# Row maxima in row tiles of the array, all row sums by additions, and a shared ring of banks

## The reference

```python
xn = _layernorm(x)                                   # x: (8, 1024, 512) float32
q, k, v = proj(Wq, bq), proj(Wk, bk), proj(Wv, bv)   # 16 heads of 32
scores = jnp.einsum('bhid,bhjd->bhij', q, k) / jnp.sqrt(32)
im = jnp.arange(L) % 256
scores = jnp.where(im[:, None] >= im[None, :], scores, -1e30)
attn = jnp.einsum('bhij,bhjd->bhid', jax.nn.softmax(scores, axis=-1), v)
s = attn.transpose(0, 2, 1, 3).reshape(B, L, D) @ Wo.T + bo
w = (weights >= 0.0) * 2.0 - 1.0
g = _silu(jnp.clip((xn @ w.T) * scale + bias, -100, 100))
out = x + s * g
```

## Time and profile before

| | |
|---|---|
| median of three runs | 1720.07 us (1716.95 to 1721.70) |
| span of the profiled execution | 1718.3 us (the profile has no time outside it) |
| PE busy | 1670.7 us, 97% |
| DVE, POOL, ACT busy | 1344.2, 1188.0, 1158.4 us |
| POOL additions L1205 | 763.9 us in 628 |
| DVE maxima L1008 | 780.6 us in 1216 |
| ACT exponentials L796 of transposed scores | 621.6 us in 1088 |

### The profile page before, as it was taken

The page is one execution under the profiler, slowest core; times in us unless marked ns, Lnnn a source line. Parts: engine busy times, 40 slices in busy tenths (PEclk is TensorE's granted clock), DMA queues, the critical chain, the costliest instruction groups (busy, mean ns, idle before and its releaser), DMA issues.

```text
span 1718.3 us, 34103 instructions
## 1 busy us (share of the span) xinstructions
PE 1670.7 (97%) x11660; PEld 781.8 (45%) x11660; DVE 1344.2 (78%) x2641; ACT 1158.4 (67%) x2734; POOL 1188.0 (69%) x1186
## 2 busy tenths in 40 slices
PE   8999999999999999999999999999999999999988
PEld 4444444444444444444444444444444444444433
DVE  6889677787778877888777877778777787777874
ACT  4577676677677765677756777666776677666763
POOL 0167667786867768777588775787757786667775
PEclk9999999999999999999999999999999999999989
DMA  7314212333123421234122331224312332122111
GB/s 212 110 39 88 69 45 63 87 89 85 34 71 92 100 57 46 68 99 100 38 63 69 104 85 37 75 63 111 76 38 64 81 99 54 42 63 75 44 51 50
DMA packets 185038, 126.09 MB, mean 73 GB/s; under 512 B 106912, under 2 KB 159264, under 8 KB 184416
## 3 DMA queue, kind: packets, MB, share of 16 engines
q1 hardware_dynamic: 183904, 123.13, 28.2%
q10 hardware_dynamic: 960, 0.79, 0.2%
HBM read 41.50 MB, written 17.05 MB: 34 GB/s over the span
## 4 chain that ended last, share of the span: by engine, by line
PE 83%; ACT 7%; DVE 5%; issue 2%; POOL 1%; DMA 1%; ACTq 0%; SPq 0%; POOLq 0%; DVEq 0%
PE pJ L496 29%; PE pO L698 15%; PE pS L655 11%; PE pT L679 10%; PE pT L675 3%; PE pJ L588 3%; PE pJ L592 3%; PE pJ L589 3%; ACT pS L808 3%; PE pS L658 3%; DVE mx L1008 2%; ACT PT L796 2%; PE pT L639 2%; PE pJ L583 1%; ACT acc L796 1%
## 5 line engine op out<-in xcount | busy, mean ns | idle before, releaser
L1008 DVE TENSOR_REDUCE mx<-pS 128x1 f32<-128x512 f32 (+3 forms) x1216 | 780.6, 656 | 258.0 <-PE pS L655 176.0
L796 ACT ACTIVATE PT<-pT 128x512 f32<-128x512 f32 (+1 forms) x1088 | 621.6, 583 | 431.1 <-PE pT L679 381.6
L1205 POOL TENSOR_TENSOR acc<-acc,PT 128x512 f32<-128x512 f32 x628 | 763.9, 1250 | 30.3 <-PE pO L698 30.3
L655 PE MATMUL pS<-QK 96*128 96x512 f16 (+3 forms) x1280 | 389.7, 318 | 20.1 <-ACT pS L808 14.5
L679 PE MATMUL pT<-QK 97*128 97x512 f16 (+3 forms) x1280 | 393.4, 318 | 4.2 <-ACT PT L796 1.6
L808 ACT ACTIVATE pS<-pS,a 128x384 f32<-128x384 f32 (+3 forms) x512 | 266.1, 524 | 13.8 <-DVE a L1023 13.4
L698 PE MATMUL pO<-PT,V 128*32 128x512 f32 (+3 forms) x2816 | 262.4, 486 | 0.2 <-ACT PT L796 0.2
L655 PEld LDWEIGHTS pS<-QK 96*128 96x128 f16 x1280 | 124.4, 98 | 166.0 <-issue 44.4
L496 PE MATMUL pJ<-xT,wh_q 128*128 128x512 f16 x512 | 191.7, 379 | 2.2 <-ACT xT L737 1.7
L496 PE MATMUL pJ<-wh_v,xT 128*128 128x512 f16 x512 | 192.5, 379 | 0.8 <-ACT V L776 0.8
L496 PE MATMUL pJ<-xT,wh_k 128*128 128x512 f16 x512 | 192.6, 381 | 0.0
(11 more groups left out here) (166 smaller groups left out, 2294.5 us busy)
## 6 DMA issues: line engine op xcount, KB each, us to landing
QK<-sg SPq DMA_DIRECT2D x756, 64.0 KB
xs<-in_x SPq DMA_DIRECT2D x60, 256.0 KB, 3.2
xr<-in_x SPq DMA_DIRECT2D x58, 256.0 KB, 3.0
out<-xr SPq DMA_DIRECT2D x58, 256.0 KB, 2.5
QK<-aT SPq DMA_DIRECT2D x256, 1.0 KB, 1.7
rq<-moved SPq DMA_DIRECT2D x132, 2.0 KB, 1.8
QK<-in_x SPq DMA_DIRECT2D x8, 256.0 KB, 4.0
QK<-in_mqk SPq DMA_DIRECT2D x2, 512.0 KB, 9.2
```

The source lines that it names most:

```text
L655: ins = e.matmul(s_bank("s", i)[:, base:base + wide], q4[0:96, j, qc], k4[0:96, j, 0:wide], start=True, stop=True)
L796: e.activation(probabilities_at(i), t_bank("t", i)[:, 0:cols], ACT.Exp, scale=SS).then_inc(s_p, 1)
L1008: e.tensor_reduce(mx[:, par, part, :].rearrange("p (j q) -> p j q", q=4)[:, heads[0]:heads[-1] + 1, qi], s_bank("s", i)[:, 0:cols].rearran ...
L1205: e.tensor_tensor(a, a, PT[:, RING_AT[i] % NPT, 0:width * len(heads)].rearrange("p (j q) -> p j q", j=len(heads)), ALU.add).then_inc(s_ap, 1)
```

## The change

- Row scores use the high halves of q and k alone, straight from `sg`: 32 features a head, so four heads lie on four 32-row tiles of the array. Batches (`BATCHES`) replace chunks: one or two query blocks of all four heads; heads 0 to 2 go to `pS`, now one tensor of three banks, head 3 to a bank of the ring that the transposed scores use. The mask of the diagonal block is a second matmul of 32 rows from `mk`. Ten batches make a group.
- DVE takes the maximum of head 3 in one reduction (`s_m3`) and of heads 0 to 2 in another (`s_m0`). The next batch waits for `s_m0`; whoever comes two turns later on the ring waits for `s_m3`.
- Every unit gets its row sums by additions and the ones-matmul. `sum_rows`, `row_shifts` and `move_sums` go. In even units POOL adds key block 1, DVE 2 and 3. `acc` is doubled, and the ring `PT` shrinks from 12 to 8 places. Additions in even units are 4 on POOL (384 columns) and 3 on DVE.
- All times of the order are new (a table `TM`). The projections of q and k of a group are issued about one group later than before.

```diff
-NPT = 12
+NPT = 8
-NPS = 3
+    for _part in range(_n % NQS + 1):
+        _diag = _part == _n % NQS
+        for _blocks in (((0, 128, 0), (1, 256, 128)), ((2, 384, 0),), ((3, 512, 0),)) if _diag else tuple(((q, 512, 0),) for q in range(4)):
+            BATCHES.append((38 * (_n // 2 - 1) + TM["s"][_n // 2 % NG][3 * (_n % NQS) + _k], (_n, _part, _diag, _blocks)))
...
-RING = [i for i, (n, kb, w, hs) in enumerate(T_TILES) if kb > 0 or n not in ADDED]
+RING = [i for i, (n, kb, w, hs) in enumerate(T_TILES) if kb > 0]
...
-    return kb >= (3 if n == NU - 1 else 4 * (n % NQS) + 2)
+    return kb >= (6 if n % NQS else 2)
...
+T_RING = sorted([(at_t(i), "t", i) for i in range(len(T_TILES))] + [(at_sums(n), "sm", n) for n in range(NU)] +
+                [(at_s(i), "s", i) for i in range(len(S_TILES))])
...
-        acc = sb("acc", [P, 4, 512], F32)
+        acc = [sb(f"acc{i}", [P, 4, 512], F32) for i in range(2)]
...
-        pS = [pb(f"pS{i}", [P, 512], F32) for i in range(NPS)]
+        pS = pb("pS", [P, 3, 512], F32)
...
-            return (s_p, j + 1) if old == "t" else (s_rt, j // 2 + 1)
+            return {"t": (s_p, j + 1), "sm": (s_rt, j + 1), "s": (s_m3, TAKEN[min(j + 1, len(S_TILES))])}[old]
...
             def row_sums():
-                for n in ADDED:
+                for n in range(NU):
...
             def scores():
...
+                    ln.wait_ge(s_qh, 4 * gn + 2 + qs + (part and 1))
+                    ln.wait_ge(s_m0, TAKEN[i])
+                    ln.wait_ge(*t_bank_free("s", i))
+                    to = [pS[:, 0, :], pS[:, 1, :], pS[:, 2, :], t_bank("s", i)[:, :]]
+                    for qi, w, c0 in blocks:
+                        q0, k0 = 512 * qs + P * qi, 512 * part
+                        for j in range(4):
+                            r = slice(32 * j, 32 * j + 32)
+                            ins = e.matmul(to[j][:, c0:c0 + w], sg[r, 0, q0:q0 + P], sg[r, 2, k0:k0 + w],
+                                           start=True, stop=not diag)
+                        if diag:
+                            for j in range(4):
+                                r = slice(32 * j, 32 * j + 32)
+                                ins = e.matmul(to[j][:, c0 + w - P:c0 + w], mk[r, 0, :], mk[r, 1, :], start=False, stop=True)
...
-            def sum_rows():
-                for i in ROW_CHUNKS:
...
             def maxima():
...
+                    yield at_s(i) + TM["mx"][0]
+                    if m > 1:
+                        ln.wait_ge(s_a16, m - 1)
                     ln.wait_ge(s_S, i + 1)
+                    for qi, w, c0 in blocks:
+                        e.tensor_reduce(mx[:, par, part, 12 + qi:13 + qi], t_bank("s", i)[:, c0:c0 + w], AX.X,
+                                        ALU.max).then_inc(s_m3, 1)
+                    yield at_s(i) + TM["mx"][1]
+                    for qi, w, c0 in blocks:
+                        e.tensor_reduce(mx[:, par, part, :].rearrange("p (j q) -> p j q", q=4)[:, 0:3, qi],
+                                        pS[:, :, c0:c0 + w], AX.X, ALU.max).then_inc(s_m0, 1)
-            def row_shifts():
...
-            def move_sums():
```

More of the change, by code:

```diff
@@ L34 @@
 I32 = mybir.dt.int32
-CHUNKS, S_LAST = [], {}
+TM = {
[13 rows of a table added]
+    "gate": (-0.5, -0.32, 2.3, 4.42, 5.25),
+    "ln": ((-51.1, -0.3, -10.79, 11.14), (-86.71, 8.09, -7.92, 8.94), (-13.68, 1.5, -2.54, 8.89)),
+    "mx": (0.24, 0.81),
+    "sh": (2.63,),
+    "stage": (-0.42, 0.3),
+    "hl": (-2.23, -1.54),
+    "pr": (0.06,),
+    "add": (2.93, 3.16),
+    "nrm": (0.23, 1.28),
+    "out": (1.17, 0.84, 1.34),
+    "hi": ((3.58, 4.05), (3.96, 3.47)),
+    "vst": (-0.27,),
+    "res": (0.1, 1.34),
+}
+BATCHES, B_LAST = [], {}
 T_TILES, T_FIRST, T_LAST = [], {}, {}
@@ L117, in at_s @@
 def at_s(i):
-    return CHUNKS[i][0]
+    return S_AT[i]
 def at_t(i):
@@ L227, in at_ln @@
     x0 = at("x", b, 4 * h)
[L228 to L231 removed]
+    t = TM["ln"][2 if h else 0 if b == 1 else 1]
+    first = x0 + t[0]
+    return first, first + t[1], t[2], first + t[3]
 def in_time(*strands):
@@ L430, in outputs_taken @@
             return (s_or, (n + 1) // 2) if n % 2 else (s_on, n + 1)
-        def row_shift(i):
-            n, _, part, _, _ = S_TILES[i]
-            return ap[:, part, :] if n == NU - 1 else a16[:, n % 2, 0:16]
         def probabilities_at(i):
             n, kb, width, heads = T_TILES[i]
-            if kb == 0 and n in ADDED:
-                return acc[:, heads[0], :]
+            if kb == 0:
+                return acc[n % 2][:, heads[0], :]
             return PT[:, RING_AT[i] % NPT, 0:width * len(heads)]
@@ L1045, in shifts @@
+                    ln.wait_ge(s_m3, TAKEN[last_batch(m) + 1])
+                    ln.wait_ge(s_m0, TAKEN[last_batch(m) + 1])
+                    if par:
                         e.tensor_tensor(mx[:, par, 0, :], mx[:, par, 0, :], mx[:, par, 1, :],
@@ L1061, in additions @@
                     n, kb, width, heads = T_TILES[i]
-                    yield at_t(i) + 8.11
-                    a = acc[:, heads[0]:heads[-1] + 1, 512 - width:512]
+                    yield at_t(i) + TM["add"][1]
+                    a = acc[n % 2][:, heads[0]:heads[-1] + 1, 512 - width:512]
                     if by_vector(n, kb):
@@ L1199, in additions @@
                     n, kb, width, heads = T_TILES[i]
-                    yield at_t(i) + 2.75
-                    a = acc[:, heads[0]:heads[-1] + 1, 512 - width:512]
+                    yield at_t(i) + TM["add"][0]
+                    a = acc[n % 2][:, heads[0]:heads[-1] + 1, 512 - width:512]
                     ln.wait_ge(s_pv, units(n) + 1)
@@ L1209, in normalise @@
                 for n in range(1, NU - 1, 2):
-                    yield past("sm", n) + (0.32 if n in ROW_AT else 0.98)
+                    yield past("sm", n) + TM["out"][2]
                     ln.wait_ge(s_R, n + 1)
```

289 lines of the change are left out of this document (88 added, 201 removed), and 13 rows, old and new, of the table TM.

## The result

The changed kernel took 1839.34 us, the median of four runs (1838.32 to 1841.86); the kernel before took 1718.61 us beside it (1716.95 to 1721.70). The ratio is 1.070 with a 95% interval of [1.0682, 1.0717]: slower by 7%, or 121 us. The prediction, 1683 us and faster, was wrong in size and in sign, and the time lies above its range.

A forecast was written before the change was run, and what follows sets the result against it. The prediction took PE, busy 97% of the span, to bound the kernel. Its terms summed as 1718.3 - 68 (PE) - 19 (ACT) + 16 (DVE) + 26 (POOL) + 8 (end) = 1681, 1683 us with 1.8 to the median; range 1632 to 1745.

The forecast's parts named there:

- What PE waited for before: PE's waits in the kernel before: small, the largest for score banks held by ACT and DVE, 14.5 and 4.8 us.
- PE's work: Row scores on PE save 3.2 us a group, added row sums cost 1.1: -68 us in all.
- the case that the row tiles work: Sign that the forecast is right: PE busy falls below 95% although its work falls by 4%.
- The estimate by the Trainium skill's figure: Row tiles on PE: by 3.07x, tiling costs 1.3 us a group instead of 2.3, time 32 us lower.
- the rival in which the covers hold: Batch gaps and POOL's additions: neither new wait is seen, 1641 us; chance 0.24.
- Rival D: Row scores on PE: the four row tiles run one after another, 1873 us; chance 0.04.
- POOL and the shorter ring: Third PV pair of odd units: exponentials late behind POOL's additions with 8 places, 0.8 us a group, +26 us.
- DVE, short gaps between batches: Row-score batches: PE waits for DVE's reductions in short gaps, 0.5 us a group, +16 us; ends 0 and 1.2.
- The clock: End of the kernel: the granted clock may add some time there; no size given.
- The end: Last unit's first addition to the kernel's end: 44.5 us instead of 36.2, +8 us.
- Rival B: Third PV pair of odd units and short batch gaps: waits take what PE gives, 1747 us; chance 0.22.

The follow-up runs named there:

- d4: Changed kernel with POOL's additions on 32 columns a head, the fourth head's row-score matmuls left out and DVE's maxima over 32 columns a block: 1655.70 us.
- b2: Changed kernel with POOL's four additions of each even unit cut to 32 columns, all waits kept: 1789.65 us.
- The ladder: Changed kernel with successively POOL's additions short, the fourth head's row-score matmuls left out, DVE's maxima short: 1839, 1726, 1700, 1656 us.
- b3: Changed kernel without DVE's three additions of each even unit: 1770.05 us.
- a2: Changed kernel with every addition on POOL cut to 32 columns a head, all waits kept: 1726.0 us.
- d5: Changed kernel with DVE's maxima over 32 columns a block, POOL's additions whole: 1789.48 us.
- c4: Changed kernel with POOL's additions on 32 columns a head and the fourth head's row-score matmuls left out: 1700.05 us.

## Why the prediction was wrong

**What PE waited for before: a misreading.** The prediction calls the score banks of ACT and DVE, 14.5 and 4.8 us, the largest waits of PE. The second largest was another, the bank of the ring of two that ACT had not emptied:

```profile
PE pT L675 <- ACT PT L796: 8.9, 14, 1.5
```

The ring of two was thus already tight before the fourth head was put into it.

**PE's work: right.** PE busy fell under 95% of the span, as forecast for the case that the row tiles work. Row tiles run side by side and a batch costs about 0.18 us more than its columns, for my 0.23. (Of the 0.23, the last 0.05 came from a pitch of 0.853 us for a pair of PV steps that no row shows; the earlier trace rows has 0.88, with which it is nothing.) In d4 PE is busy 86.7 us less than before, about 80 with the fourth head added, at a granted clock of 0.995 against 0.994; I had taken off 68. (The estimate by the Trainium skill's figure, 32 us lower, charged each mask like a block of 512. Over the 2.41 us of columns in a group the ratio 4 / 3.07 adds 0.7 us, which makes it 50 us lower.) With the three sources of lateness taken away (d4) the kernel takes 1656 us where the rival in which the covers hold had 1641. Rival D, row tiles one after another, is excluded by the four starts within 0.01 us.

**POOL and the shorter ring: the step that failed.** I took 26 us, with 3 us a group (96 us) as the upper end; with POOL's additions short the kernel takes 113 us less, of which the four new additions of an even unit alone are 50 (b2). The price was read at one place only, the exponential of key block 5 that needs the twelfth addition, and for one mechanism, the ring. Both were the wrong ones: ACT's wait for POOL is 26.9 us where the prediction wanted well over 31.8, and ten places for eight give 4 us, within noise. POOL's lateness goes other ways. The first is the even unit: its four additions were costed as POOL time (4.1 us of about 50, "no bound as a sum"), and its ones-matmul as 1.1 us of PE, but not as a wait at the head of PE's queue behind two engines; without DVE's additions there, 69 to 75 us go, DVE's freed time with them. The second is ACT's queue, where the gate's tanh waits for POOL and exponentials stand behind it. In the earlier trace rows a gate stood between additions too, and what stood behind it on ACT had not been asked.

**DVE, short gaps between batches: mis-sized.** I took 16 us for DVE's answer and the shared bank together, with 1.2 us a group (38 us) as the upper end. The ladder gives 44 and 26, by themselves 50 and 9. The gaps were counted as if DVE were free when a batch ended, with 0.7 us for an addition. DVE's busy time was to fall by 0.6 us a group, 19 us in all, and rose by 96 (1344.2 to 1440.6). Its additions take 980 ns apiece; in b3, where only those of odd units are left, they take 784, so those of even units took about 1.18 us (an estimate, (188.1 - 75.3) / 96). How much each of these adds to the time was not measured. The start of the kernel belongs here: PE is busy 82.05 us of the first 100 in the changed kernel, 83.82 with POOL's additions short (a2), 86.82 with the maxima short (d5) and 89.92 in d4, where it was 90.30 before.

**The clock: no term.** I named it for the end of the kernel alone. By the two estimates above it took 50 to 60 us of the 184 that lie between d4 and the changed kernel.

**The end: right.** The last unit's first addition starts at 1794.27, and from there to the end are 43.9 us, for 44.5 predicted.

```profile
1794.27 10.24 POOL L1157 TENSOR_TENSOR acc<-acc,PT 128x512 f32<-128x512 f32 x8
```

**Rival B** (waits take what PE gives, 1747 us) had the right sign, and of its conditions PE without slack; the other did not come, three engines at over 80% (POOL 73%, DVE 78%, ACT 50%). It was still 92 us short. It took 3.3 us a group from the same two places; their upper ends, 3 and 1.2, would have given 1776 us, which is short as well. What it lacked was the even unit's link and the clock. The Trainium skill (TensorEngine Tiling (Array Packing), PSUM Bottleneck) warns that after the speedup the emptying of PSUM may be the bottleneck; the trace agrees in part: with DVE's maxima short (d5) at most 50 us of the 183 go, and POOL, which empties no bank here, was worth more than twice as much.

What is left open: how the 72 us of the odd units divide between the gates on ACT's queue, the ring of eight and DVE's slower work was not tried apart; and whether a wholly new order could hide the even unit's link, since every single shift tried made the time longer.

## What to carry to other kernels

When an engine at 97% gives away work, ask of each added dependency what stands at the head of an in-order queue while it is unmet, on every engine that it passes, and not only whether the engine has the time in sum: 4.1 us of additions a group on an engine at 69% cost about 50 us over the kernel, 1.6 a group. Look at the chain that ended last before the busy shares: it named POOL where the shares named nobody. Price a wait of the matmul engine at up to one and a half times its length when it is otherwise busy, since the clock can fall behind it (here 119 us of idle time came with an estimated 50 to 60 us of slower matmuls). And moving a late instruction, or giving it to an idle engine, is safe only if it waits for nothing there and nothing waits for it: four such moves each cost 45 to 77 us.

## What the runs showed of the hardware

Four 32-row tiles into four banks start within 0.01 us and cost 0.23 us for 512 columns, against 0.217 for a single matmul: 3.8 times (4 x 0.217 / 0.23). That leaves out the 0.18 us for going in and out; a lone block of 512 columns with both comes to 2.1 times (an estimate, 0.868 / 0.41). The Trainium skill (TensorE: Matmul & The Clock Gate, Part 3, Measured speedup vs the span model) has 3.07, by which the prediction estimated 0.28 us for a block; the block of 512 columns in the trace takes 0.23, and by the estimate here a lone one with its two changes of tiling 0.41.

DVE's operations with two inputs in SBUF, the on-chip memory, take longer beside POOL's long additions. The subtraction L969 (128x512, L976 before and L968 in d4), by shape (columns as the earlier trace rows); before, then changed, then d4:

```profile
L976 DVE TENSOR_TENSOR HL<-xs,HL 128x512 f16<-128x512 f32 x56 | 57.4, 1035 | 10.6 <-ACT HL L729 9.1
```

```profile
L969 DVE TENSOR_TENSOR HL<-xs,HL 128x512 f16<-128x512 f32 x56 | 80.5, 1466 | 7.6 <-ACT HL L738 7.3
```

```profile
L968 DVE TENSOR_TENSOR HL<-xs,HL 128x512 f16<-128x512 f32 x56 | 48.9, 892 | 39.8 <-ACT HL L737 39.7
```

With POOL's additions short it takes 876 to 892 ns (a2, c4, d4), with them whole 1035 to 1466. POOL's busy share does not foretell it: 1035 ns at 69% (before), 1466 at 73% (changed) and 1114 at 75% (d5). A small operation shows it most. The addition L1014 over 16 elements takes 167 or 168 ns in a2 and d4 and 485 in the changed kernel:

```profile
L1014 DVE TENSOR_TENSOR mx<-mx 128x16 f32<-128x16 f32 x32 | 15.5, 485 | 0.2
```

The maxima, which read PSUM, do not change: L1003 over 1536 elements takes 1744 ns with POOL's additions whole or short. The Trainium skill (GPSIMD Engine Reference, Specifications) lists POOL's memory interfaces as shared with VectorE, with contention for two memory inputs, and the trace agrees. POOL does not explain all of DVE's slower additions: I had used 0.7 us, they took 717 ns before, with POOL at 69%, and in a2, with POOL's additions short, they still take 870. Why is open.
